# A four-layer graph network on one core: the first norm's passes spread between its end rows, the first layer's adds and maxima later behind the gathers

## The reference

```python
h = jnp.maximum(_layernorm(x, axis=-1), 0.0)
# layer 0: W_msg is (128, 64); target is sorted
edge_feats = jnp.concatenate([h[source], h[target]], axis=-1)
messages = jax.nn.relu(edge_feats @ W_msg + b_msg)
agg_sum = jax.ops.segment_sum(messages, target, num_segments=num_nodes)
# layer 1: norm = deg_inv_sqrt[source] * deg_inv_sqrt[target]
aggregated = jax.ops.segment_sum(h[source] * norm[:, None], target, num_segments=num_nodes)
```

## Time and profile before

| what | us |
|---|---|
| median of 3 runs | 5620.78 (5613.98 to 5626.88) |
| the profiled execution's own time | 5624.62 |
| its span, from the first to the last instruction | 5622.8 |
| PE busy | 3387.3 (60%) |
| POOL busy | 2834.5 (50%) |
| DVE busy | 2719.4 (48%) |
| ACT busy | 1086.5 (19%) |

### The profile page before, as it was taken

One profiled execution on the slowest core, in us unless ns is written; L12 is line 12 of the kernel. 1 busy time (PEld: TensorE's weight loads), 2 busy tenths in 40 slices (PEclk: granted clock), 3 DMA queues, 4 the chain that ended last, 5 costly groups with the idle time before them and its releaser, 6 DMA issues. The chain is left out here.

```text
span 5622.8 us, 58211 instructions
## 1 busy us (share of the span) xinstructions
PE 3387.3 (60%) x12060; PEld 2043.7 (36%) x12060; DVE 2719.4 (48%) x6625; ACT 1086.5 (19%) x2025; POOL 2834.5 (50%) x2360
## 2 busy tenths in 40 slices
PE   3664544444499577675667665777744555555534
PEld 1222433433477466552222223555531222222212
DVE  6996551111155422364555453777774444444423
ACT  0232320101122111121222222333321111111100
POOL 0462017777511584234777772122126888787740
PEclk7776555555555555555555555555556777676765
DMA  5222430010155210252111112121112222233210
GB/s 192 82 69 100 179 118 19 19 20 20 39 151 157 52 22 13 99 210 72 23 23 23 23 23 79 70 98 79 72 61 33 30 29 30 28 31 29 28 17 3
DMA packets 350982, 346.67 MB, mean 62 GB/s; under 512 B 264934, under 2 KB 290267, under 8 KB 350835
## 3 DMA queue, kind: packets, MB, share of 16 engines
q1 hardware_dynamic: 229596, 272.37, 14.8%
q0 software_dynamic: 107888, 60.13, 8.7%
q10 hardware_dynamic: 13350, 12.40, 0.6%
HBM read 172.86 MB, written 175.50 MB: 62 GB/s over the span
## 5 line engine op out<-in xcount | busy, mean ns | idle before, releaser
L825 PE MATMUL e_ps<-e_msg,e_hot 128*128 x2408 | 553.9, 421 | 449.4 <-POOL e_msg L750 324.9
L825 PEld LDWEIGHTS e_ps<-e_msg,e_hot 128*128 128x128 f32 x2408 | 526.5, 330 | 522.9 <-issue 522.9
L2208 POOL DMA_INDIRECT out<-d_out,d_end x356 | 592.6, 1665 | 172.0 <-issue 167.1
L2252 PE MATMUL d_pl<-d_hot,d_fields 128*65 128x512 f32 x712 | 501.8, 870 | 0.0
L800 DVE TENSOR_TENSOR e_ps<-e_ps,e_before 128x65 f32<-128x65 f32 (+1 forms) x172 | 40.0, 233 | 871.0 <-PE e_ps L825 871.0
L736 POOL DMA_INDIRECT e_msg<-from_src,e_src x200 | 208.0, 1040 | 374.3 <-DMA e_first<-lot_first 320.3
L1971 POOL DMA_INDIRECT list<-s_rec,s_place x200 | 197.7, 988 | 290.6 <-DVE s_place L1887 234.7
L1671 POOL TENSOR_TENSOR u_tg<-u_t,norms 128x1792 f32<-128x1792 f32 x14 | 55.5, 3964 | 441.6 <-DVE u_t L1506 441.6
L1309 PE MATMUL u_po<-bias_parts,ones 3*128 3x256 bf16 x392 | 148.8, 380 | 213.7 <-issue 95.9
L741 POOL DMA_INDIRECT e_msg<-h1d,e_src x200 | 223.5, 1118 | 101.8 <-issue 54.9
L915 POOL DMA_INDIRECT a_ends<-h,a_src x200 | 220.7, 1104 | 102.7 <-issue 60.6
(11 more groups left out here) (359 smaller groups left out, 8152.6 us busy)
## 6 DMA issues: line engine op xcount, KB each, us to landing
u_z<-h SPq DMA_DIRECT2D x28, 896.0 KB, 6.2
x<-sums SPq DMA_DIRECT2D x28, 896.0 KB, 7.8
u_x<-x SPq DMA_DIRECT2D x28, 896.0 KB, 7.4
terms<-s_zeros SPq DMA_DIRECT2D x16, 812.5 KB, 11.8
s_key_row<-src_key SPq DMA_DIRECT2D x50, 256.0 KB
h1d<-u_h SPq DMA_DIRECT2D x14, 910.0 KB, 9.4
u_z<-h1d SPq DMA_DIRECT2D x14, 910.0 KB, 4.6
term<-u_h SPq DMA_DIRECT2D x14, 910.0 KB, 3.6
```

The source lines that it names most:

```text
L825: last = nc.tensor.matmul(to, hot[s][:, q, :], rows, start=False, stop=q == LOT - 1)
L2208: pool.indirect_dma_start(net.out[:, :], bass.IndirectOffsetOnAxis(ap=end[s][:, j:j + 1], axis=0), out[s][:, j, 0:C], None, bounds_check=N ...
L2252: last = nc.tensor.matmul(pl[0:WEIGHT + 1, :], fields[:, j, :], hot[:, j, :], start=j == 0, stop=j == J - 1)
```

## The change

In first_norm the same passes are made in another order. DVE's step becomes total, FD add 0, centre, FD adds 1 and 2, sum of squares, FD adds 3 and 4, reciprocal and H, FD adds 5 and 6. ScalarE's square goes from the head of its step behind the second FS copy.

In edge_sums of layer 0 POOL adds two chunks behind the gathers and takes the maximum three chunks behind. The drain between them is gone; the maximum waits on the count of adds instead. There are three near buffers and three gathered semaphores in place of two. Layer 1 keeps its order on POOL.

In both layers PE reads the plan of a lot ahead: the first before the loop, and the next after the fourth matmul of the lot at hand.

```diff
-                def centre(c):
+                def total(c):
                     r, s, h = c
                     v.wait_ge(loaded[s], 16 * h + 16)
                     nc.vector.tensor_reduce(mean[s][:, :], X[s][:, :, :], AX.X, ALU.add)
+
+                def centre(c):
+                    r, s, h = c
                     v.drain()
...
                 def step(c, done):
-                    if c is not None:
-                        centre(c)
-                    if done is not None:
-                        from_dst(done, range(0, 3))
-                    if c is not None:
-                        variance(c)
-                    if done is not None:
-                        from_dst(done, range(3, SUBS))
-                    if c is not None:
-                        scale(c)
+                    for part, subs in ((total, (0,)), (centre, (1, 2)), (variance, (3, 4)), (scale, (5, 6))):
+                        if c is not None:
+                            part(c)
+                        if done is not None:
+                            from_dst(done, subs)
...
                 def step(c, done, start=False):
-                    if c is not None:
-                        square(c)
                     if done is not None:
                         turn_copy(done, 0, start)
...
                             from_src(done, i)
-                        if i == 3 and c is not None:
+                        if i == 1 and c is not None:
+                            square(c)
+                        elif i == 3 and c is not None:
                             root(c)
...
-            near = [sb(f"near{s}", [P, J, C]) for s in range(2)]
-        AHEAD = 2
+            near = [sb(f"near{s}", [P, J, C]) for s in range(3)]
+        AHEAD = 3 if two else 2
...
-                def finish(c):
+                def landed(c):
                     pool.wait_ge(gathered[c % AHEAD], 16 * (2 if two else 1) * J * (c // AHEAD + 1))
+                    return msg[:, J * c:J * (c + 1), 0:C]
+
+                def add(c):
+                    rows = landed(c)
+                    nc.gpsimd.tensor_tensor(rows, rows, near[c % 3][:, :, :], ALU.add).then_inc(added, 1)
+
+                def positive(c):
                     rows = msg[:, J * c:J * (c + 1), 0:C]
-                    if two:
-                        nc.gpsimd.tensor_tensor(rows, rows, near[c % 2][:, :, :], ALU.add).then_inc(added, 1)
-                        pool.drain()
-                        nc.gpsimd.tensor_scalar(rows, rows, 0.0, None, ALU.max).then_inc(msg_ready, 1)
...
-                for c in range(CHUNKS):
-                    if two and c > 1:
-                        pool.wait_ge(added, c - 1)
-                    gather(c)
-                    if c > 0:
-                        finish(c - 1)
-                finish(CHUNKS - 1)
+                    pool.wait_ge(added, c + 1)
+                    nc.gpsimd.tensor_scalar(rows, rows, 0.0, None, ALU.max).then_inc(msg_ready, 1)
...
+                if two:
+                    for c in range(CHUNKS + 3):
+                        if c < CHUNKS:
+                            if c > 2:
+                                pool.wait_ge(added, c - 2)
+                            gather(c)
+                        if 2 <= c < CHUNKS + 2:
+                            add(c - 2)
+                        if c > 2:
+                            positive(c - 3)
...
-                for g in range(LOTS):
-                    s = g % 2
+                def read_lot(g):
                     path = pe.value_load(plan[0:1, g:g + 1], min_val=0, max_val=(1 << BLOCK_BITS + LOT - 1) - 1)
                     blocks = item_blocks(pe, path)
                     slots = [pe.snap((blocks[0] + q - b).with_bounds(min_val=0, max_val=LOT - 1)) for q, b in enumerate(blocks)]
-                    chunk = pe.snap((blocks[-1] >> 2) + 1)
+                    return blocks, slots, pe.snap((blocks[-1] >> 2) + 1)
+                lot = read_lot(0)
+                for g in range(LOTS):
+                    s = g % 2
+                    blocks, slots, chunk = lot
                     pe.wait_ge(placed, g + 1)
...
                         last = nc.tensor.matmul(to, hot[s][:, q, :], rows, start=False, stop=q == LOT - 1)
+                        if q == LOT // 2 and g + 1 < LOTS:
+                            lot = read_lot(g + 1)
```

More of the change, by code:

```diff
@@ L737, in gather @@
                                                     bass.IndirectOffsetOnAxis(ap=src[:, b:b + 1], axis=0)).then_inc(gathered[c % AHEAD], 16)
-                            pool.indirect_dma_start(near[c % 2][:, j, :], None, net.from_dst[:, :],
+                            pool.indirect_dma_start(near[c % 3][:, j, :], None, net.from_dst[:, :],
                                                     bass.IndirectOffsetOnAxis(ap=dst[:, b:b + 1], axis=0)).then_inc(gathered[c % AHEAD], 16)
@@ L742, in gather @@
                                                     bass.IndirectOffsetOnAxis(ap=src[:, b:b + 1], axis=0)).then_inc(gathered[c % AHEAD], 16)
-                def finish(c):
+                def landed(c):
                     pool.wait_ge(gathered[c % AHEAD], 16 * (2 if two else 1) * J * (c // AHEAD + 1))
-                    rows = msg[:, J * c:J * (c + 1), 0:C]
-                    if two:
-                        nc.gpsimd.tensor_tensor(rows, rows, near[c % 2][:, :, :], ALU.add).then_inc(added, 1)
-                        pool.drain()
-                        nc.gpsimd.tensor_scalar(rows, rows, 0.0, None, ALU.max).then_inc(msg_ready, 1)
-                    else:
-                        factor = msg[:, J * c:J * (c + 1), C:C + 1].to_broadcast([P, J, C])
-                        nc.gpsimd.tensor_tensor(rows, rows, factor, ALU.mult).then_inc(msg_ready, 1)
@@ new lines, in positive, with scale @@
+                def positive(c):
+                    rows = msg[:, J * c:J * (c + 1), 0:C]
+                    pool.wait_ge(added, c + 1)
+                    nc.gpsimd.tensor_scalar(rows, rows, 0.0, None, ALU.max).then_inc(msg_ready, 1)
+                def scale(c):
+                    rows = landed(c)
+                    factor = msg[:, J * c:J * (c + 1), C:C + 1].to_broadcast([P, J, C])
+                    nc.gpsimd.tensor_tensor(rows, rows, factor, ALU.mult).then_inc(msg_ready, 1)
+                if two:
[8 more added lines that the diff above has]
+                            positive(c - 3)
+                else:
+                    for c in range(CHUNKS):
+                        gather(c)
+                        if c > 0:
+                            scale(c - 1)
+                    scale(CHUNKS - 1)
```

## The result

The changed kernel took 5453.22 us (median of 4 runs, 5451.18 to 5462.3) beside 5619.1 us for the kernel before (4 runs, 5613.98 to 5626.88). The ratio is 0.9704, with a 95% interval from 0.9692 to 0.9715. The profiled execution took 5462.3 us, its span is 5460.5, its mean granted clock 0.575, as before. The direction was right; the gain is 166 us where 117 had been forecast, and the time lies 22 us under the range.

The account below looks back on a forecast made before the run. Barrier-separated stages, no engine at peak; POOL paced the first edge sums, PE the second layer's. 5624.6 - 75 (first norm) - 42 (first edge sums) = 5507.6, or 5504 against the median; range 5475 to 5570.

Parts of the forecast that it names:

- the collisions: First edge sums: POOL gathers lengthened by DVE's one-hot comparisons; kept the same, at most +24 us.
- The 55: First edge sums: 55 us of longer gathers in the stage, from means of 1.136 and 1.040 against 0.95 us.
- PE's reading of the plan: Lots of both layers: moving the 0.75 us load gains 0 us, since PE's sequencer is the bound.
- the hidden load: Rival, second layer: the plan's load hides behind matmuls, a lot takes 3.93 us; 5440 us, chance 0.08.
- the arithmetic made twice: Rival, PE's lots: register arithmetic made again in mid-lot, up to 2.14 us a lot; 5705 us, chance 0.06.
- POOL's gap: First edge sums: idle time before each maximum shrinks from 1.26 to 0.1 us in 48 gaps, -55.7 us.
- The tail: End of first edge sums: PE still runs eight lots after the last gather, from 1436.1 to 1474.3.
- The first norm: First norm: passes placed among PE's products bring the step from 20.6 to 14.5 us, -75 us.
- The transfers: Rival, first norm: transfers hold the step at 17.5 us; 5542 us, chance 0.12.
- a denser POOL meets the lock more often: First edge sums: POOL without gaps meets DVE's shared port lock more often, at most 24 us.

Follow-up runs that it names:

- e2: The kernel before with only PE's reading ahead of the plan in mid-lot; 5590.32 us, ratio 0.9935.
- e4: The changed kernel with a POOL drain put back behind each add; 5519.3 us, ratio 0.9805.
- e1: The kernel before with only the first norm's new order; 5541.45 us, ratio 0.9851.
- e3: The kernel before with only POOL's new order, the drain gone; 5579.29 us, ratio 0.9916.
- e6: The changed kernel with POOL's add and maximum one chunk behind the gathers, the maximum waiting on its own add; 5601.96 us on a slower chip, ratio 0.9689.

## Why the prediction was right and where it was wrong

- **The step that failed** is the one on the collisions: "There are still 86 comparisons, released by POOL's maxima as before, so I keep it the same". Their number and their release are the same, and 31 us of gather time went all the same, since what counts is which of two starts comes first. (The 55 were nearer 50: the first gather of each chunk takes 1.04 us with no comparison near it.) The two starts had been 0.04 us apart, at the very edge, and the change moved the comparison by 0.3. The bounds were wrong as well: up to +24 was allowed, and nothing below zero. The row that the text itself quoted, 1139.35 against 1139.39, was the place to ask on which side of the gather the comparison would land. e2 alone shows the term, at a ratio of 0.9935 for an edit priced at 0.
- **PE's reading of the plan**: right in its own mechanism. PE stops 0.3 us in mid-lot and gains it back (3.52 and 0.60 to 0.76 for 3.22 and 0.91), lots stay at 4.70 on chips A and B, and neither the hidden load (5440) nor the arithmetic made twice (5705) came. What failed was to take 0 for the edit because PE's pace stays: that same stop of 0.3 us had been foreseen, and not followed to the comparison that hangs on the lot's end.
- **POOL's gap**: right, mis-sized by a little. 0.1 us was forecast and 0.0 measured; e4 puts the drain back and with it 60.2 us. From first to last gather it is -94.3 us where -58 had been forecast: about -61 for the gaps, -2.5 for the order and -31.0 for shorter gathers.
- **The tail**: right. Eight lots behind the last gather, 38.1 us where 38.2 had been worked out (1436.1 to 1474.3).
- **The first norm**: right, mis-sized by 7 us: 13.98 a step and not 14.5. The five steps whose restart is at the low clock are 14.3 to 14.5 long, as laid out from durations of the low clock (with the normed rows 0.35 us sooner and the restart 0.3 longer than laid out); the other eight restart at the fast clock and are 13.7, which makes some 6 of the 7 us. Which steps do so differs between executions (6 of 13 in e1), so that part is not the kernel's alone. The transfers (5542) held nothing at 239 GB/s.
- The sum of the missed terms: 8 up to the first gather, 31 for the collisions, about 5 for the gap, 1 in all the rest and 4 between profiled executions and medians, together 49 us: 166 less 117.

The Trainium skill (SBUF — State Buffer, "SBUF: two separate sides") was cited ahead for the lock between DVE and GpSimd's descriptors. The held gathers (1.87 us for 0.95) agree with it in kind. The same section says that whichever of the two starts first gets the shared pair for its whole instruction; the border at 0.034 us agrees, and this was the part that the forecast did not use. In two points these traces differ from the section, and the measurements decide. It says that its probe did not see a `tensor_tensor` stall a DMA, and the comparison here is one. And it says that the one that comes second is fully blocked, while a gather that started first leaves the comparison its 1.08 us. That a denser POOL meets the lock more often was the forecast's own inference; e3 has the denser POOL and 62 slow gathers against 61, so it does not here.

The opening of this document says that the engines meet only through semaphores. The held gathers, adds and maxima show that DVE and POOL also meet without one.

What stays open: why, in the same changed kernel, the second comparison falls mostly on an eighth gather on chip A (24 held gathers, no held maximum) and more often on an add and its maximum on C and D (15 and 17 held gathers, 12 and 11 held maxima). No run isolates that, nor what makes these chips slower.

## What to carry to other kernels

Where two engines collide in some of their instructions, look at the distance between the two starts, not at their count: with 0.04 us between them, a shift of 0.3 us anywhere ahead, even of work that costs nothing by itself, is worth 30 us or takes them. Price such an edit from both sides, and put the phase on the list of what it may move. Count the collisions on every instruction that can have one: e6 seems nearly free of them if only gathers are counted. Where a mean mixes two clocks, as in the steps of the norm, compare the repetitions at the same clock. And a drain between two operations of one queue may wait for much more than the first of them: a wait on that operation's own count cost 0.09 us where the drain cost 1.2.

## What the runs showed of the hardware that was not expected

- DVE's comparison (128x896, both operands in SBUF, 1.08 us) holds a gather of POOL only if it started at least 0.034 us ahead of it; the gather then ends 0.81 to 0.84 us behind the comparison, however far that had come (1.86 us for a gather that starts 0.04 behind it, 1.19 for one 0.71 behind). The other way round neither is longer: the comparison that started 0.28 us into a gather took 1.08 us.
- Against POOL's own arithmetic both are longer. In e6 a comparison that starts inside an add takes 1.3 to 1.5 us, and the maximum that follows takes 1.58 us and not 0.84. Maxima with no comparison beside them have a median of 0.84 to 0.87 us on all chips.
- The drain on POOL behind eight indirect transfers and an add left 1.0 to 1.8 us idle before the maximum in e4 (and 2.26 behind the last gather), also where the maximum's own add was a round old. Behind an add alone it left 0.19.
- The same products of PE, eight passes, took 0.72 us at a granted clock of 1.00 and 1.23 at 0.50, and a norm step 13.7 or 14.5 us, by whether PE resumed inside a stretch of the fast clock.
